# A deformable convolution stack on one core: window and offset loads re-laid, sums and residual once per band

## Chip, cores and metric

The kernel runs on 1 core of one Trainium2 chip. The metric is the device time of one launch in microseconds, lower is better; a time is the median of several runs.

## The reference

Eight images of 32 channels and 64 x 64 pixels are normalised, and pass through four blocks (a 3 x 3 convolution h = relu(conv(x)), a 3 x 3 convolution of h that gives 18 offsets per pixel, and a deformable convolution of h at these offsets), with residuals between the blocks. A final deformable convolution takes the result and the normalised input together (64 channels). All is float32.

```python
off = offset.reshape(Bn, K * K, 2, Hh, Ww)
py = base_y + off[:, :, 0]
px = base_x + off[:, :, 1]
sampled = jax.vmap(_bilinear_sample)(x, py, px)      # weights max(0, 1-|d|) of the four neighbours
return jnp.einsum('bckhw,ock->bohw', sampled, wk) + b
...
x = _block(x, deconv_w[0], ...)
in_prev = jnp.zeros_like(x)
for i in range(1, 4):
    in_cur = x + in_prev
    x = _block(in_cur, deconv_w[i], ...)
    in_prev = in_cur
x_cat = jnp.concatenate((x, in_module), axis=1)
offset = _conv2d(x_cat, fin_off_w, fin_off_b, PAD)
return _deform_conv2d(x_cat, offset, fin_dcn_w, fin_dcn_b)
```

## The kernel before

**Partition of the work.** The images are two groups of four; the 128 partitions are 4 images x 32 channels. Each of the four layers, and the final step, is done for one group after the other: ten steps in all. In a step the convolutions run first (`conv_tiles`, L467), the map h is transposed and stored to DRAM as `ht_store` (row, column, channels of four images; L330), and the scaled positions (offset plus tap) go through `FOFF` to DRAM as `off_store` (L339). VectorE reduces the positions to their range, and flags choose the kind of sampling: kind 0 (windows of 11 x 11 positions) ran in the eight steps of the layers, kind 1 (16 x 16 positions in two tiles of 128) in the two final ones. Then comes the call of sampling (`sampling`, L241), between barriers of all five engines.

**A call of sampling.** An image is 16 bands of 4 rows, a band two chunks of 32 columns (`half` 0 and 1), so 32 chunks; a chunk is 8 blocks of 4 x 4 pixels. `chunk_loop` (L254) writes the first and the last chunk out and loops over pairs of chunks between them. The bilinear weights are made as hats of a distance, and sampling becomes a matrix product of a window (positions on the partitions) with the weights of all its positions. Per chunk:

- SP loads the positions: `load_offsets` (L348), eight transfers per band for both halves, each to 16 partitions (`HB`), the source repeated 16 times. `load_windows` (L357) loads 11 transfers per chunk (16 in the final steps), one per window row, from `ht_store` to `VT`, in runs of 128 numbers (256 in the final steps).
- ScalarE: the distance |HB - position| of the next chunk (L693), VectorE clamps it (L844), GpSimd splits it into two fp16 hats (L998, L1000) that TensorE will read as `HL`.
- For each of 12 groups (three taps of one image), TensorE spreads the x hats and the y hats over the window positions (`spread`, L492, two matmuls each, times two tiles for y in kind 1) into the PSUM banks `P[2*slot]` and `P[2*slot+1]` of three slots; ScalarE copies x to `XC` (L707), VectorE multiplies y by it into `A` (L828).
- In between, TensorE samples the chunk before (`sample`, L505, matmuls of `A` and `VT` into one of the two banks of `PS`, two blocks per part); ScalarE reads each part into `SMP` (L676). After the last part the sums over the nine taps (`deform`, L523) run in two pieces, 128 columns wide; ScalarE applies bias and activation into `TMP` (L665), VectorE adds the residual into `X` (L822).

**What sets the order.** Each engine's program is written out by hand with semaphores. PE runs in order: `self.after` says after which group the parts of the chunk before are sampled, `self.sum_spots` where the pieces of the sums stand. PE may be at most three groups ahead of VectorE (`product_done`, credit of `SLOTS`). SP's queue is in order as well: in the loop over bands it waits until the second half of `HB` has been read, issues the eight offset loads of the next band, then waits for `ps_full` and issues the windows of the two chunks.

```python
src = bass.AP(off_store.ap().tensor, at, [[0, ROWS], [CH * CPX, 2], [1, TAPS * CPX]])
q = CH * i + ROWS * axis
sp.dma_start(HB[q:q + ROWS, :, :], src).then_inc(hb_full, 16)
```

"Units" are the two halves of the rows in the convolutions; "a part" is one sampling product group; "spread" means the matmul of the selection table `SEL` with the hats.

Of the kernel before, what the change touches and what calls it, by code (L numbers as in the profile page):

```python
# [14 lines left out]
IMG = 4  # L15
# [14 lines left out]

MARGIN = 6
HP = SIDE + 2 * MARGIN

XSIZE = (SIDE + 2) * HP
ROWS = 16
# [8 lines left out]

SHEETS = UNIT_ROWS * HP // 128
BANKFULS = (SHEETS + 3) // 4
# [7 lines left out]

class Shape:

    def __init__(self, kind, sources):
# [4 lines left out]

        self.batches = 2 if kind == 1 else 1
# [5 lines left out]
        self.parts = [(w, s) for w in range(0, self.blocks, 2) for s in range(sources)]  # L71

        runs = [2, 5] if len(self.parts) < 8 else [1, 3, 5, 7]
        count = len(self.parts) // len(runs)
        self.after = {g: list(range(count * n, count * (n + 1))) for n, g in enumerate(runs)}
        self.sum_spots = [8, 10] if len(self.parts) < 8 else [9, 10]

        self.read_after = {g + 1 + k: n for g in runs for k, n in enumerate(self.after[g])}
        self.out_after = 11
        self.ps_uses = self.batches * len(self.parts) + 1  # L80
        assert self.ps_uses % 2 == 1 and len(self.read_after) == len(self.parts)

def build(nc, t):

    ctx = ExitStack()
    with ctx:
# [3 lines left out]
        def sem(name):  # L91
# [5 lines left out]
        ht_store = [nc.dram_tensor(f"ht_store{n}", (HP, HP, n, 128), F32) for n in (1, 2)]  # L97

        SLOTS = 3  # L100
# [4 lines left out]
        XC = sb("XC", [128, SLOTS, 3 * CPX])  # L105
        SMP = sb("SMP", [128, 2, 2, TAPS * CPX])
        TMP = sb("TMP", [128, 2, CPX])
# [17 lines left out]
        P = ctx.enter_context(nc.psum_tensor("P", [128, 6, 512], F32))  # L125
        PS = ctx.enter_context(nc.psum_tensor("PS", [128, 2, 512], F32))
# [32 lines left out]
        hb_full = sem("hb_full")  # L159
# [3 lines left out]
        hats_full = sem("hats_full")  # L163
        x_full = sem("x_full")
        x_ready = sem("x_ready")
        y_full = sem("y_full")
# [7 lines left out]
                    flag_step, hb_full, abs_done, clamp_done, hat_step, hats_full, x_full, x_ready, y_full, product_done,  # L174
                    *vt_full, ps_full, ps_free, res_done, turn]

        credit = [(x_ready, SLOTS), (product_done, SLOTS), (y_full, 1), (ps_full, 2), (ps_free, 2), (res_done, 2), (turn, 1)]
# [13 lines left out]
        def bankful(unit, n):  # L191

            return SHEETS * unit + 4 * n, min(4, SHEETS - 4 * n)

# [4 lines left out]
        def bank(n):  # L199
            return P[:, n, :] if n < 6 else PS[:, n - 6, :]  # L200
# [8 lines left out]
        def smp_px(buf, source, w, blocks):  # L209
            return SMP[:, buf, source, 144 * w:144 * (w + blocks)]  # L210

# [17 lines left out]
        BARS = 4  # L229
# [11 lines left out]
        def sampling(eng, bar_count, final, body, fallback, clears=False):  # L241
# [5 lines left out]
            with eng.If(kind == 1):  # L247
                body(Shape(1, sources))
            with eng.If(kind > 1):
                fallback(Shape(2, sources))  # L250
            barrier(eng, bar_count + 1)
            clear_step(eng, bar_count + 2, clears)
# [36 lines left out]
        def _(sp):  # L289
# [40 lines left out]
            def store_ht(sources, s, unit, n):  # L330
                sp.wait_ge(ht_copied, (UNITS * s + unit) * BANKFULS + n + 1)
                first, count = bankful(unit, n)
                at = (MARGIN * HP + 128 * first) * sources * 128 + 128 * s
                dst = bass.AP(ht_store[sources - 1].ap().tensor, at,
                              [[sources * 128, 128], [128 * sources * 128, count], [1, 128]])
                sp.dma_start(dst, staged(s)[:, 128 * first:128 * (first + count)].rearrange(
                    "p (t c) -> p t c", c=128)).then_inc(ht_stored, 16)
# [761 lines left out]
```

## Time and profile before

| | us |
|---|---|
| median of 3 runs | 6885.23 |
| lowest, highest | 6860.79, 6908.06 |
| the profiled execution | 6814.77 |
| its span | 6813.0 |

| engine | busy us (share) |
|---|---|
| PE matmuls | 5270.7 (77%) |
| PE weight loads | 3746.3 (55%) |
| DVE (VectorE) | 2989.2 (44%) |
| ACT (ScalarE) | 2803.4 (41%) |
| POOL (GpSimd) | 1134.7 (17%) |

The granted clock of TensorE is 0.796 of the full one over the span. The span is the time from the first to the last instruction; the profiled execution's own time is a little longer. "Busy" is the time in which an engine executed; a line as "L693" is a line of the kernel; "<-" names what an engine's idle time ended with. "issue" is idle time that ends with no releaser in the profile. SPq is the queue in which SP issues transfers. In a window, PEclk is the granted clock as a share of the full one and "DMA share" the mean busy share of the 16 DMA engines (it can pass 1 where packets overlap).

### The profile page before, as it was taken

To read this page: it belongs to the slowest core of one execution; us is meant where nothing else is said; L and a number is where in the kernel's file an instruction comes from. 1 tells how busy PE (TensorE), PEld (TensorE's weight loads), DVE (VectorE), ACT (ScalarE), POOL (GpSimd) and SP (SyncE) were. 2 spreads that over 40 slices of the span, in tenths; PEclk is the share of its full clock that TensorE was granted. 3 is DMA by queue.
4 is the path that set the end of the run, shared out by engine and by line. 5 is a ranking of instruction groups with operands and counts; after the bars stand their busy time and mean duration, and the time that the engine had idled before them with its cause. 6 is when DMAs were issued, how large, how long until landed. Compare 5 with 4: busy or idle time off the path is not lost.

```text
span 6813.0 us, 210332 instructions
## 1 busy us (share of the span) xinstructions
PE 5270.7 (77%) x73160; PEld 3746.3 (55%) x73160; DVE 2989.2 (44%) x5831; ACT 2803.4 (41%) x7035; POOL 1134.7 (17%) x655
## 2 busy tenths in 40 slices
PE   3888688688688768868858868876777777678887
PEld 2555455355455545545535545554656566566776
DVE  3444454355355345445535534533334342344444
ACT  1554354255355345435525525542323232233333
POOL 0221222122022122112202202211101010111110
PEclk8778787688788878878868877887788788788888
DMA  5553553355255255345435525547666665778875
GB/s 152 75 75 56 79 80 60 70 80 81 56 77 79 57 79 78 55 81 81 71 65 78 78 56 77 77 91 106 78 77 84 79 80 83 116 91 96 96 90 77
DMA packets 615113, 544.03 MB, mean 80 GB/s; under 512 B 90160, under 2 KB 570160, under 8 KB 613040
## 3 DMA queue, kind: packets, MB, share of 16 engines
q1 hardware_dynamic: 614576, 536.57, 53.3%
q8 instruction: 374, 6.13, 0.5%
q14 instruction: 163, 1.34, 0.1%
HBM read 468.16 MB, written 68.12 MB: 79 GB/s over the span
## 4 chain that ended last, share of the span: by engine, by line
PE 51%; issue 21%; DMA 12%; ACT 6%; SPq 4%; DVE 3%; ACTq 1%; POOL 1%; POOLq 0%; PEldq 0%; PEld 0%; DVEq 0%
PE P L502 20%; PE PS L516 17%; PE PS L528 13%; DMA HB<-off_store 11%; SPq L355 4%; ACT SMP L676 2%; DVE A L828 2%; ACT XC L707 2%; ACT DIST L693 2%; PE P L474 1%; ACTq L704 0%; DMA H<-gn_store 0%; DMA gn_store<-X 0%; POOL HL L1000 0%; DMA X<-x_dram 0%
## 5 line engine op out<-in xcount | busy, mean ns | idle before, releaser
L828 DVE TENSOR_TENSOR A<-P,XC 121x384 f32<-121x384 f32 (+1 forms) x4608 | 2412.5, 555 | 3006.6 <-ACT XC L707 1595.6
L707 ACT ACTIVATE XC<-P 121x384 f32<-121x384 f32 (+1 forms) x4608 | 1961.1, 443 | 2903.3 <-PE P L502 2876.1
L502 PE MATMUL P<-HL,SEL 32*121 32x384 f16 (+1 forms) x21504 | 2355.4, 345 | 835.7 <-POOL HL L1000 393.6
L502 PEld LDWEIGHTS P<-HL,SEL 32*121 32x121 f16 (+1 forms) x21504 | 1341.2, 132 | 1632.7 <-issue 879.8
L516 PE MATMUL PS<-A,VT 121*32 121x144 f32 (+1 forms) x32768 | 1467.0, 335 | 124.1 <-issue 95.1
L516 PEld LDWEIGHTS PS<-A,VT 121*32 121x32 f32 (+1 forms) x32768 | 1098.5, 127 | 468.4 <-issue 238.0
L528 PE MATMUL PS<-SMP,CW 128*128 128x128 f32 x6912 | 1100.3, 316 | 301.7 <-ACT SMP L676 300.9
L528 PEld LDWEIGHTS PS<-SMP,CW 128*128 128x128 f32 x6912 | 963.6, 219 | 529.5 <-ACT SMP L676 428.2
L998 POOL CAST HL<-DIST 128x1152 f16<-128x1152 f32 x320 | 366.2, 1144 | 4394.1 <-DVE DIST L844 4110.0
L1000 POOL TENSOR_TENSOR HL<-DIST,HL 128x1152 f16<-128x1152 f32 x320 | 760.0, 2375 | 129.7 <-issue 73.9
L676 ACT ACTIVATE SMP<-PS 128x288 f32<-128x288 f32 x1536 | 639.2, 416 | 24.0 <-PE PS L516 22.7
L693 ACT ACTIVATE DIST<-HB,CONST 128x1152 f32<-128x1152 f32 x320 | 402.8, 1259 | 593.8 <-DMA HB<-off_store 593.7
L844 DVE TENSOR_SCALAR DIST<-DIST 128x1152 f32<-128x1152 f32 x320 | 240.2, 751 | 161.7 <-ACT DIST L693 161.7
L474 PE MATMUL P<-X,DW 32*32 32x512 f32 x3456 | 165.5, 682 | 158.6 <-DMA CW<-dcn_w_dram 120.3
L474 PE MATMUL P<-H,OW 32*32 32x512 f32 x3456 | 227.8, 684 | 35.1 <-DVE FOFF L927 35.1
L769 ACT ACTIVATE H<-P,BIAS 32x512 f32<-32x512 f32 x128 | 87.9, 686 | 258.5 <-PE P L474 225.6
L474 PEld LDWEIGHTS P<-H,OW 32*32 32x32 f32 x3456 | 131.3, 110 | 110.9 <-issue 80.1
L474 PE MATMUL PS<-H,OW 32*32 32x512 f32 x2304 | 189.0, 719 | 0.0
L474 PEld LDWEIGHTS P<-X,DW 32*32 32x32 f32 x3456 | 80.6, 109 | 193.8 <-issue 179.7
L1006 POOL PARTITION_ALL_REDUCE ST<-ST x10 | 3.9, 391 | 1088.3 <-DVE ST L950 1088.3
L927 DVE SCALAR_TENSOR_TENSOR FOFF<-P,PXB 128x512 f32<-128x512 f32 x48 | 32.9, 685 | 299.6 <-PE PS L474 188.6
L822 DVE SCALAR_TENSOR_TENSOR X<-X,CONST,TMP 128x128 f32 (+1 forms) x320 | 110.6, 346 | 65.5 <-ACT TMP L665 65.5
(55 smaller groups left out, 826.4 us busy)
## 6 DMA issues: line engine op xcount, KB each, us to landing
HB<-off_store SPq DMA_DIRECT2D x1280, 144.0 KB, 5.7
VT<-ht_store SPq DMA_DIRECT2D x1024, 128.0 KB
VT<-ht_store SPq DMA_DIRECT2D x2816, 44.0 KB
ht_store<-A SPq DMA_DIRECT2D x80, 256.0 KB, 3.6
off_store<-FOFF SPq DMA_DIRECT2D x160, 128.0 KB, 2.5
ht_store<-H SPq DMA_DIRECT2D x6, 1444.0 KB, 19.4
A<-x_dram SPq DMA_DIRECT2D x2, 2048.0 KB, 10.9
gn_store<-X SPq DMA_DIRECT2D x2, 2048.0 KB, 26.3
```

Source lines behind the costliest of these rows:

```text
L355: sp.dma_start(HB[q:q + ROWS, :, :], src).then_inc(hb_full, 16)
L474: mm = nc.tensor.matmul(bank(bank0 + i)[CH * j:CH * (j + 1), :], weights[q, CH * k:CH * (k + 1)], view(row + k // 3 - 1, col + k % 3 - 1)[ ...
L502: mm = nc.tensor.matmul(dst, SEL[q, table, 0:sh.npos], hats, start=part == 0, stop=part == 1)
L516: mm = nc.tensor.matmul(out[q, 144 * v:144 * v + 144].rearrange("p (k y x) -> p k y x", k=TAPS, y=BLK), vt_tile(sh, vt_buf, n, 0 if same_w ...
L528: mm = nc.tensor.matmul(out[:, 0:CPX], CW[:, s, 128 * k:128 * (k + 1)], rhs, start=n == 0, stop=n == len(products) - 1)
L676: nc.scalar.activation(smp_px(0, s, b * sh.blocks + w, 2), PS[:, (half + use) % 2, 0:288], ACT.Copy).then_inc(ps_free, 1)
L693: nc.scalar.activation(DIST[:, :], HB[:, half, :], ACT.Abs, bias=HAT_BIAS).then_inc(abs_done, 1)
L707: nc.scalar.activation(XC[0:sh.npos, slot, 0:sh.size], P[0:sh.npos, 2 * slot, 0:sh.size], ACT.Copy).then_inc(x_ready, 1)
L828: return nc.vector.tensor_tensor(dst, y, x, ALU.mult)
L844: nc.vector.tensor_scalar(DIST[:, :], DIST[:, :], SCALE, SCALE, ALU.min, ALU.subtract).then_inc(clamp_done, 1)
L998: nc.gpsimd.tensor_copy(HL[:, 0, half, :], DIST[:, :]).then_inc(hat_step, 1)
L1000: nc.gpsimd.tensor_tensor(HL[:, 1, half, :], DIST[:, :], HL[:, 0, half, :], ALU.subtract).then_inc(hats_full, 1)
```

## The change

- **Windows.** `ht_store` is laid out in four lanes: columns 0, 4, 8, ... of the padded map in the first, 1, 5, 9, ... in the second, and so on. The eight blocks of a chunk are four columns apart, so a window position's eight values are now one contiguous run (1024 numbers, 2048 in the final steps). A chunk's windows are four transfers, one per lane. The positions stand on the partitions in the order of lanes, and the tables `REL` and `SEL` follow. The transposes of h write lanes (20 instead of 19 per unit).
- **Offsets.** The y axis has 16 rows of the store and the x axis the next 16, so that one transfer per image and half fills 32 partitions of `HB`; its source is 2 axes x 16 repeats x 1152 numbers. Each half has its own semaphore, and the load of a chunk is issued when the distance two chunks earlier has run. The first band's loads, its first distance, clamp and hats stand ahead of the barrier of the step; they are issued after the first unit's offsets are stored, ahead of the stores of the second unit.
- **PSUM.** Three banks for the operand that ScalarE copies (now y) and four for the one that VectorE reads (now x), one bank for samples and sums instead of two.
- **Parts and sums.** Three parts per chunk of 3, 3 and 2 blocks (kind 0) instead of four of 2; six parts instead of eight in the final steps. Sums, activation and residual run once per band, over both chunks: 9 products of 256 columns (18 in the final steps), after group 10 of the first chunk of the next band.
- One barrier less per step, and nested branches instead of three in a row.

```diff
-            def load_offsets(band):
+            def load_offsets(band, half):
                 for i in range(IMG):
-                    for axis in range(2):
-                        at = band * BAND_SIZE + (i * 2 * CH + axis * TAPS) * CPX
-                        src = bass.AP(off_store.ap().tensor, at, [[0, ROWS], [CH * CPX, 2], [1, TAPS * CPX]])
-                        q = CH * i + ROWS * axis
-                        sp.dma_start(HB[q:q + ROWS, :, :], src).then_inc(hb_full, 16)
+                    at = band * BAND_SIZE + (2 * i + half) * CH * CPX
+                    src = bass.AP(off_store.ap().tensor, at, [[AXIS * CPX, 2], [0, AXIS], [1, TAPS * CPX]])
+                    sp.dma_start(HB[CH * i:CH * (i + 1), half, :], src).then_inc(hb_full[half], 16)
-            def load_windows(sh, buf, corner):
-                for r in range(sh.win):
-                    tile, first = divmod(r, sh.win // sh.tiles)
-                    src = bass.AP(ht_store[sh.sources - 1].ap().tensor, corner + r * (HP * sh.sources * 128),
-                                  [[sh.sources * 128, sh.win], [BLK * sh.sources * 128, BLOCKS], [1, sh.sources * 128]])
...
+            def load_windows(sh, buf, corners):
+                width = sh.sources * 128
+                size = BLOCKS * width
+                for corner, (tile, first, columns) in zip(corners, sh.lanes):
+                    src = bass.AP(ht_store[sh.sources - 1].ap().tensor, corner, [[LANE_COLS * width, sh.win], [width, columns], [1, size]])
+                    sp.dma_start(VT[first:first + sh.win * columns, buf, tile * size:(tile + 1) * size], src).then_inc(vt_full[buf], 16)
...
-                load_offsets(0)
-                load_windows(sh, 0, corner(0, 0))
-                with sp.Fori(0, BANDS - 1) as band:
-                    sp.wait_ge(abs_done, 2 * band + 2)
-                    load_offsets(band + 1)
-                    free_windows(2 * band + 1)
-                    load_windows(sh, 1, corner(band, 1))
-                    free_windows(2 * band + 2)
-                    load_windows(sh, 0, corner(band + 1, 0))
+                load_windows(sh, 0, corners(0, 0))
+                load_windows(sh, 1, corners(0, 1))
+                next_offsets(2, 1, 0)
+                next_offsets(3, 1, 1)
+                with sp.Fori(0, BANDS - 2) as pair:
+                    next_offsets(2 * pair + 4, pair + 2, 0)
+                    next_windows(pair + 1, 0)
+                    next_offsets(2 * pair + 5, pair + 2, 1)
+                    next_windows(pair + 1, 1)
...
+                    if unit == 0:
+                        for slot in range(OFF_SLOTS):
+                            sp.wait_ge(off_stored[slot], 32)
+                        load_offsets(0, 0)
+                        load_offsets(0, 1)
...
-        P = ctx.enter_context(nc.psum_tensor("P", [128, 6, 512], F32))
-        PS = ctx.enter_context(nc.psum_tensor("PS", [128, 2, 512], F32))
+        P = ctx.enter_context(nc.psum_tensor("P", [128, Y_SLOTS + X_SLOTS, 512], F32))
+        PS = ctx.enter_context(nc.psum_tensor("PS", [128, 512], F32))
...
+                    rhs = SMP[:, first:first + chunks, 0:sh.smp_size].rearrange(
+                        "p h (w s k a) -> p h w s k a", s=sh.sources, k=TAPS, a=BPX)[:, :, :, s, k, :]
+                    mm = nc.tensor.matmul(PS[:, 0:chunks * CPX], CW[:, s, 128 * k:128 * (k + 1)], rhs,
...
+                distance(0, 0)
                 sampling(act, bar_count, final, lambda sh: body_of(sh, final), lambda sh: fallback_of(sh, final))
...
                 for n in range(ITEMS):
                     unit, image = divmod(n, IMG)
+                    if n == IMG:
+                        clamp(0)
```

SP, in the loop over bands of a layer's sampling, before; a row is one instruction with the shape of its destination, `ISA` a register or wait instruction:

```order
L355 ISA [waits abs_done]
L355 DMA HB<-off_store 16x2x1152
...
L380 ISA
L364 ISA [waits ps_full]
L364 DMA VT<-ht_store 11x8x128
```

The same place now:

```order
L372 ISA [waits abs_done]
L372 DMA HB<-off_store 32x1x1152
...
L402 ISA
L380 ISA [waits ps_full]
L380 DMA VT<-ht_store 33x1x1024
```

The eight offset loads of a band, in one piece, became four for each half, each four with a wait of its own and the windows of one chunk behind them; the eleven windows became four (three of 33 partitions and one of 22).

PE, in the first chunk of the loop, one part of samples between two groups of spreads, and a piece of the sums, before:

```order
L516 MATMUL PS<-A,VT 32x144 [waits ps_free]
L516 MATMUL PS<-A,VT 32x144 x7
L564 REGISTER_ALU
...
L528 MATMUL PS<-SMP,CW 128x128 [waits ps_free]
L528 MATMUL PS<-SMP,CW 128x128 x3
L564 REGISTER_ALU
```

Now, in the second chunk of the loop:

```order
L549 MATMUL PS<-A,VT 32x144 [waits ps_free]
L549 MATMUL PS<-A,VT 32x144 x11
...
L583 REGISTER_ALU
L562 MATMUL PS<-SMP,CW 128x256 [waits ps_free]
L562 MATMUL PS<-SMP,CW 128x256 x8
L590 REGISTER_ALU
```

A part is now three blocks in 12 matmuls, and the sums of both chunks stand in one piece of nine, where each chunk had a piece of four and one of five.

## Rows read from the trace of the kernel before

**Rows 1.** Distances (L693) of three sampling calls: count, ns min/median/max, first to last start.

```profile
L693 ACT ACTIVATE DIST<-HB,CONST x32: 1246/1255/1282, 2958.6 to 3388.7; 128x1152 f32<-128x1152 f32 x32
...
L693 ACT ACTIVATE DIST<-HB,CONST x32: 1245/1251/1256, 4644.3 to 5688.7; 128x1152 f32<-128x1152 f32 x32
...
L693 ACT ACTIVATE DIST<-HB,CONST x32: 1246/1251/1256, 5850.6 to 6740.1; 128x1152 f32<-128x1152 f32 x32
```

**Rows 2.** Windows, one period of four chunks in a layer.

```profile
core 0: us, PE busy (x) PEld busy (x) DVE busy (x) ACT busy (x) POOL busy (x), PEclk, DMA share, GB/s
3093.90:3128.10 34.20, 28.89 (x360) 19.40 (x356) 19.42 (x39) 21.93 (x52) 7.68 (x5) 1.00 0.67 92
3128.10:3148.50 20.40, 19.29 (x168) 12.19 (x165) 9.39 (x19) 8.79 (x21) 6.56 (x4) 0.50 0.32 59
```

**Rows 3.** Timeline of the same chunks, ACT and SP: start, us, what [idle before].

```profile
3100.94 1.27 ACT L693 ACTIVATE DIST<-HB,CONST 128x1152 f32<-128x1152 f32 x1
...
3112.24 1.27 ACT L693 ACTIVATE DIST<-HB,CONST 128x1152 f32<-128x1152 f32 x1
...
3113.70 3.83 SPq L355 DMA_DIRECT2D HB<-off_store  x8
...
3125.35 1.25 ACT L693 ACTIVATE DIST<-HB,CONST 128x1152 f32<-128x1152 f32 x1 [1.66 <-DMA HB<-off_store]
...
3141.49 1.25 ACT L693 ACTIVATE DIST<-HB,CONST 128x1152 f32<-128x1152 f32 x1
```

**Rows 4.** Timeline of one chunk at the full clock, PE.

```profile
3104.24 1.19 PE L516 MATMUL PS<-A,VT 121*32 121x144 f32 x32
...
3107.46 1.16 PE L528 MATMUL PS<-SMP,CW 128*128 128x128 f32 x8 [1.09 <-ACT SMP L676]
...
3109.35 1.38 PE L528 MATMUL PS<-SMP,CW 128*128 128x128 f32 x10
3110.66 0.89 PE L502 MATMUL P<-HL,SEL 32*121 32x384 f16 x12
```

**Rows 5.** Timeline in the first final call, SP and PE.

```profile
5142.88 9.28 SPq L364 DMA_DIRECT2D VT<-ht_store  x16
...
5164.22 4.05 PE L516 MATMUL PS<-A,VT 128*32 128x144 f32 x59 [9.15 <-issue]
```

**Rows 6.** Waits of PE in the two final calls: us, times, longest.

```profile
PE P L502 <- issue: 148.6, 29, 9.0
PE PS L516 <- issue: 89.4, 12, 9.4
...
PE P L502 <- issue: 107.5, 15, 11.3
```

**Rows 7.** Windows with offset loads, loads of x, and window loads (final).

```profile
3114.50:3125.00 10.50, 9.12 (x122) 6.26 (x124) 6.68 (x14) 5.73 (x15) 3.52 (x2) 1.00 0.99 128
13.00:24.00 11.00, 0.00 (x0) 0.00 (x0) 10.63 (x18) 0.20 (x1) 0.00 (x0) 1.00 1.02 398
5143.00:5161.00 18.00, 11.07 (x175) 9.24 (x170) 6.45 (x13) 4.76 (x17) 0.00 (x0) 0.94 1.12 122
```

**Rows 8.** The page, DMA packets and the issues of the loads.

```profile
DMA packets 615113, 544.03 MB, mean 80 GB/s; under 512 B 90160, under 2 KB 570160, under 8 KB 613040
...
HB<-off_store SPq DMA_DIRECT2D x1280, 144.0 KB, 5.7
VT<-ht_store SPq DMA_DIRECT2D x1024, 128.0 KB
VT<-ht_store SPq DMA_DIRECT2D x2816, 44.0 KB
```

**Rows 9.** Timeline between two calls of sampling, before the first chunk.

```profile
3496.39 0.69 DVE L927 SCALAR_TENSOR_TENSOR FOFF<-P,PXB 128x512 f32<-128x512 f32 x1 [11.57 <-PE PS L474]
...
3510.10 3.63 SPq L355 DMA_DIRECT2D HB<-off_store  x8
...
3521.18 1.25 ACT L693 ACTIVATE DIST<-HB,CONST 128x1152 f32<-128x1152 f32 x1 [41.06 <-DMA HB<-off_store]
```

More of the change, by code:

```diff
@@ L53 @@
 BAND_SIZE = IMG * 2 * CH * CPX
+AXIS = 16
 class Shape:
@@ L63, in __init__ @@
         self.npos = self.win * self.win // self.tiles
+        if kind == 0:
+            self.lanes = [(0, 33 * j, 3 if j < 3 else 2) for j in range(LANES)]
+        else:
+            self.lanes = [(j // 2, 64 * (j % 2), 4) for j in range(LANES)]
         self.batches = 2 if kind == 1 else 1
@@ L70, in __init__, with use @@
         self.size = 3 * self.px
[L71 to L81, printed above, removed]
+        units = [(w, s) for w in range(self.blocks) for s in range(sources)]
+        count = {4: 2, 8: 3, 16: 6}[len(units)]
+        edges = [(len(units) * n + count - 1) // count for n in range(count + 1)]
+        self.parts = [units[a:b] for a, b in zip(edges, edges[1:])]
+        self.after = {2: [3, 7], 3: [2, 5, 8], 6: [0, 2, 4, 5, 7, 8]}[count]
+        self.sum_after = 10
+        self.chunk_uses = self.batches * count
+        self.band_uses = 2 * self.chunk_uses + 1
+        self.smp_size = BLOCKS * sources * TAPS * BPX
+    def use(self, band, half, n=0):
+        return band * self.band_uses + half * self.chunk_uses + n
 def build(nc, t):
@@ L158, in build @@
         flag_step = sem("flag_step")
-        hb_full = sem("hb_full")
+        hb_full = [sem(f"hb_full{i}") for i in range(2)]
         abs_done = sem("abs_done")
@@ L246, in sampling @@
                 body(Shape(0, sources))
[L247 to L252, printed above, removed]
+            with eng.Else():
+                with eng.If(kind == 1):
+                    body(Shape(1, sources))
+                with eng.Else():
+                    fallback(Shape(2, sources))
+            clear_step(eng, bar_count + 1, clears)
         def chunk_loop(eng, body, tail):
@@ L503, in spread, with sample @@
                 return mm
-            def sample(sh, a_buf, vt_buf, first, w, source, out, same_window=False):
-                for v in range(2):
+            def sample(sh, a_buf, vt_buf, first, units, same_window=False):
+                for v, (w, source) in enumerate(units):
                     for n in range(sh.tiles):
@@ L695, in body, with read_sum, next_distance @@
+                def read_sum(band):
+                    act.wait_ge(ps_full, sh.use(band, 2) + 1 + PS_CREDIT)
+                    act.wait_ge(res_done, band + 2)
+                    out_act(final, 2 * BLOCKS).then_inc(ps_free, 1)
+                def next_distance(c, band, half):
+                    wait_alone(act, hats_full, c)
+                    distance(band, half)
                 def body(c, band, half, first, last):
-                    if first:
-                        distance(0, 0, 0, True)
@@ L867, in body @@
                                 clamp(c + 1)
-                            if not first and b == sh.batches - 1 and g == (11 if sh.kind == 0 else 1):
-                                add_residual(c - 1, band + half - 1, 1 - half)
+                            if half == 0 and not first and b == sh.batches - 1 and g == (11 if sh.batches == 1 else 1):
+                                add_residual(band - 1)
                 def tail():
-                    add_residual(CHUNKS - 1, BANDS - 1, 1)
+                    add_residual(BANDS - 1)
                 chunk_loop(dve, body, tail)
```

334 lines of the change are left out of this document (164 added, 170 removed).

## The prediction

> **What bounds the kernel now.** I read the start times of the distance step first, because there is one per chunk and so they are a clock of the work; then the windows of one period, the waits, and the DMA views. A layer's call of sampling takes 430.1 us from its first distance to its last, 31 chunks of 13.9 us. The two final calls take 1044.4 and 889.5 us, 33.7 and 28.7 us a chunk [rows 1]. Eight calls of the first kind are 3,440 us, the two final ones 1,934: sampling is four fifths of the 6813 us.
>
 At the full clock a chunk takes 11.3 us, in which PE has four groups of spreads of 0.89, two of samples of 1.19 and two of sums of 1.16 and 1.38, together 8.5 us [rows 4]; the rest is PE waiting for ScalarE and VectorE, for instance 1.09 us ahead of the sums.
>
> In the final calls PE stops for 5 to 11 us at a time with nothing named as releaser, 238.0 us in the first call and 107.5 in the second [rows 6]. The stop that ends at 5164.22 after 9.15 us lies at the end of window loads that were issued from 5142.88 on [rows 5]; they carry 16 times 128 KB, and at the 122 GB/s of that window this is 17 us [rows 7, 8]. I read these stops as PE's own instructions arriving late behind the window data.
>
> **The offset loads.** This is the largest term, and it speaks against the change. Before, a band takes eight loads of 16 by 2 by 1152, now each chunk takes four of 32 by 1152, with a source whose outer count is 2 (the two axes), then 16 repeats. The bytes are the same, 590 KB a chunk. How many of the 16 DMA engines share a transfer can be counted. Each transfer ends with one 4-byte write per engine. There are 5443 transfers: 1280 of offsets, 1024 and 2816 of windows [rows 8], 323 others. If each ended on 16 engines, there would be 87,088 such writes; if the 2816 whose rows are 11 on both sides end on 11, there are 73,008. Add the other short packets (16,384 of 256 B from the two stores of x, 768 of constants) and it is 90,160, exactly the count under 512 B [rows 8]. So a transfer is dealt out by its outer count. No transfer of before has a 2 there. Dealt by the source's count of 2, the new loads run on two engines; dealt by the destination's 32, on sixteen. I take two, since an engine can't be given part of an outer step in any transfer that I can count. The Trainium skill, in DMA: Bandwidth & Descriptors, section Why a DMA increments its semaphore by 16 and not by 1, says that the number is the largest up to 16 that divides the outer sizes of both sides, and that it is the lowest-numbered engines; by that it is two, always the same ones. The count above agrees for 11 and 16 and shows nothing of 2 against 32.
>
> What two engines give: while x is loaded, 16 engines move 398 GB/s, 24.9 each; in an offset load of before all 16 move 128 GB/s, 8.0 each, all of them on one source row at a time [rows 7]. Two engines alone ask for 50 GB/s, far under the 128, so I take 24.9 and keep 8.0 as the far end. Each of the two carries 64 runs of 4608 B per chunk, and of the windows 11 runs of 4096 B (three columns in three loads, two in the last), 340 KB. That is **13.7 us a chunk** at 24.9 GB/s, 42 us at 8.0. It is double-buffered by halves: the load of a chunk is issued when the distance two chunks earlier has run, so the two engines are never without work. SP is not in the way: it issues 8 transfers a chunk instead of 15, and its wait for a distance holds back only windows that are needed a chunk later. The distances then follow each other at 13.7 us, whatever PE could do.
>
> **What else the layers gain, and what hides it.** The sums run once per band with 256 columns instead of twice with 128: between no gain (columns decide) and 2.5 us per band (weight loads decide); three reads of PSUM instead of four, one activation and one residual per band instead of two; four product slots instead of three, so that PE's samples no longer stop VectorE. Without transfers I would put a chunk at 10.3 us at the full clock, between PE's 8.5 and the 11.3 of now. All of it lies under the 13.7 us of the two engines and is worth nothing there. At half the clock PE needs up to 17 us for a chunk and could be last again for a chunk, but it catches up afterwards, so the mean stays near 13.7; I allow 0.8 us for it in the range. Waits of 3 us per chunk will keep the clock falling.
>
> Per layer call: the chunk-0 distance and hats are now ahead of the barrier. Before, loads were issued at 3510.10 and that distance ran at 3521.18 [rows 9], PE some 5 us later. But the two halves of band 0 take 2 x 11.8 us on two engines, VectorE's clamp of chunk 0 now stands ahead of the second unit's offsets (3496.39 now [rows 9]), and the second unit's stores queue behind them. I put the start of PE at about 3522 instead of 3526, a gain of 4 of a possible 13. The load for chunk 2 lands some 18 us later (3.6 of windows, 11.8 of offsets, 2 of start), at 3540; 29 more at 13.7 bring the last distance to 3937, 416 us after where the first one was, against 430. With 4 us for the last chunks and one barrier less, a call saves 18 us: **8 x 18 = 144 us**.
>
> **The final calls.** Chunks are 24 us and more, so 11.8 us of offsets don't bind. The windows of a chunk come in four transfers with runs of 8 KB instead of 16 with 1 KB. On all 16 engines the 2 MB take 17 us now [rows 7]; at between 398 and half of that they take 5 to 11. If fetched instructions wait behind them, stops of 9 us shrink to the 3 to 4 us of the shortest. The first call has 41 stops for 238 us, the second 15 for 107.5 [rows 6]. Saved per call, at 3.5 us each that stay: 94 and 55 us, and a third as much again in less time at the low clock; sums, reads and the wider ring give 1 to 1.5 us of a 24 us chunk, some 40 us per call. **280 us** for both, between 80 (stops stay) and 450 (they vanish).
>
> **Sum.** The profiled execution took 6814.8 us (span 6813.0). Less 144, 280 and 10 for the two final starts, it gives 6381. The median of the runs is 6885.2, 70 above the profiled one: **6450 us**.
>
> **Rivals.** (1) The loads are spread over 16 engines after all. Then a chunk's 725 KB take 5.7 us at 128 GB/s, hidden; no distance waits, the clock stays up, and a layer chunk takes 10.6 us: 3.3 us less for 248 chunks is 820, the starts give 100 more, the final calls 350: 6885 - 1270 = 5615. For it: the destination has 32 rows; against it: the count of 11. (2) Slower: the two engines are slower than 24.9 GB/s on these runs, with the same DRAM rows read 16 times, as the 8.0 in a crowd shows. It decides from 15.5 us a chunk (21.9 GB/s), where 1.8 us more for 248 chunks has eaten the 434. At 18 us a chunk it costs 4.3 x 248 = 1070: 7520. (3) The stops in the final calls are not from the window data and stay: 200 us of the gain are gone, 6650. (4) The stop at the low clock feeds itself, and a layer chunk takes 14.8: 6450 + 270 = 6720.
>
> **Chances.** Forecast 0.50, (1) 0.14, (2) 0.13, (3) 0.12, (4) 0.11. The likeliest case has 6250 to 6650 for itself. To leave out at most 2 in 10 the range reaches to 5750 and to 6950. About 1% can be told from no change here. Faster by more than 1%: 0.80, within 1%: 0.06, slower: 0.14.
>
> **What would show it.** Right: 4-byte writes for the offset loads that count 2 each, distances 13.5 to 14 us apart in the layers with waits for HB of 2 to 4 us ahead of nearly every one, a DMA share of all 16 engines under 0.3 there, and PE and VectorE idle behind ScalarE; in the final calls, stops under 5 us. The forecast is wrong if the distances of a layer come under 12 us or over 15, or if the waits for HB are gone.

## The result, and the profile after

| | before | after |
|---|---|---|
| median, us (4 runs each) | 6873.01 | 6303.22 |
| lowest to highest | 6830.16 to 6908.06 | 6294.74 to 6315.18 |
| profiled execution, us | 6814.77 | 6309.22 |
| mean granted clock | 0.796 | 0.798 |

The ratio is 0.9175, with a 95% interval of 0.9118 to 0.9232: the kernel became 8% faster. Some executions of a kernel fall into a slower state with a lower granted clock; ratios here and below are of the other executions alone, so they are not always the quotient of two medians. The two profiled executions differ by 505.5 us; the prediction had 434.

The distances of the same three calls as in [rows 1], now L698:

```profile
L698 ACT ACTIVATE DIST<-HB,CONST x32: 1247/1258/1284, 2854.6 to 3285.2; 128x1152 f32<-128x1152 f32 x32
...
L698 ACT ACTIVATE DIST<-HB,CONST x32: 1245/1255/1288, 4488.9 to 5383.9; 128x1152 f32<-128x1152 f32 x32
...
L698 ACT ACTIVATE DIST<-HB,CONST x32: 1245/1262/1292, 5512.5 to 6236.0; 128x1152 f32<-128x1152 f32 x32
```

The layer's call shown still takes 430.6 us for 31 chunks, where it took 430.1; over the eight calls the mean chunk went from 14.0 to 13.9 us. The final calls fell from 1044.4 and 889.5 us to 895.0 and 723.5.

The page, DMA packets and the issues of the loads, against [rows 8]:

```profile
DMA packets 233565, 542.39 MB, mean 86 GB/s; under 512 B 40240, under 2 KB 141360, under 8 KB 215216
...
HB<-off_store SPq DMA_DIRECT2D x1280, 144.0 KB
VT<-ht_store SPq DMA_DIRECT2D x256, 512.0 KB
VT<-ht_store SPq DMA_DIRECT2D x768, 132.0 KB
VT<-ht_store SPq DMA_DIRECT2D x256, 88.0 KB
```

The count of short packets settles how the offset loads are dealt out. With two closing writes for each of the 1280 loads, 11 for the 1024 window loads of the layers (768 and 256), 16 for the 256 of the final calls and for the 323 others, there are 23,088; with the 17,152 short packets of x and the constants this is 40,240, the number of the page. So each offset load runs on two engines. The rule of the Trainium skill that the prediction named (DMA: Bandwidth & Descriptors, section Why a DMA increments its semaphore by 16 and not by 1) is borne out for 2 against 32, which no transfer of before could show. Which two engines they are, no view shows.

The DMA view of 50 us in a layer call. Each digit is the busy share of the 16 engines in tenths, under it what they moved:

```profile
DMA  4211111114452111111124441111111544111111
GB/s 149 98 52 52 52 52 52 52 49 143 141 153 91 52 52 52 52 52 51 52 78 152 132 157 52 52 52 52 52 50 52 154 141 157 68 52 52 52 55 52
```

No slice is empty. Between the window loads the strip stands at 1 tenth, two engines of 16, at 52 GB/s: 26 each. In the trace's records of packets some load is in flight at every moment of this call after its first 32 us. This queue doesn't run dry.

One would now expect ScalarE to wait ahead of each distance. It doesn't. The timeline of ScalarE, SP and PE in some chunks of the same call (start, us, what, idle before):

```profile
3018.29 1.26 ACT L698 ACTIVATE DIST<-HB,CONST 128x1152 f32<-128x1152 f32 x1
...
3031.38 1.27 ACT L698 ACTIVATE DIST<-HB,CONST 128x1152 f32<-128x1152 f32 x1
...
3043.15 1.25 ACT L698 ACTIVATE DIST<-HB,CONST 128x1152 f32<-128x1152 f32 x1 [3.10 <-DMA HB<-off_store]
...
3045.09 1.67 PE L549 MATMUL PS<-A,VT 121*32 121x144 f32 x24 [4.74 <-DMA VT<-ht_store]
...
3054.97 5.60 PE L562 MATMUL PS<-SMP,CW 128*128 128x256 f32 x18 [0.23 <-ACT SMP L707]
...
3062.18 1.28 ACT L698 ACTIVATE DIST<-HB,CONST 128x1152 f32<-128x1152 f32 x1
...
3070.75 1.25 ACT L698 ACTIVATE DIST<-HB,CONST 128x1152 f32<-128x1152 f32 x1
```

The distances follow at 13.1, 11.8, 19.0 and 8.6 us. A wait for offsets comes once in several chunks:

```profile
ACT DIST L698 <- DMA HB<-off_store: 355.6, 62, 21.1
```

In the call shown it is 37.8 us in seven waits, 21.1 of them ahead of the first distance. There is a new wait: PE waits 4.74 us for windows (105.2 us in 68 waits in the whole run). I read these as windows that queue behind the offsets on the two engines; with the offsets over 16 engines, below, no such wait is left. The windows of three whole chunks:

```profile
3062.20:3070.80 8.60, 7.53 (x113) 5.09 (x112) 7.17 (x14) 7.25 (x18) 3.53 (x2) 1.00 0.17 64
3070.80:3089.10 18.30, 16.72 (x133) 10.60 (x130) 7.12 (x15) 7.63 (x19) 3.52 (x2) 0.63 0.26 88
2963.80:2976.90 13.10, 11.95 (x133) 8.22 (x131) 7.04 (x15) 7.57 (x19) 3.53 (x2) 1.00 0.25 82
```

A chunk without sums takes 8.6 us at the full clock, one with sums 13.1 at the full clock or 18.3 when the clock is granted at 0.63. Two answers therefore fit a mean of 13.9: the two engines' queue, or the clock. The experiments are for that.

### The profile page after: what moved, and what is told of

The parts are those of the page before. It is cut to its first block, busy times and chain, and to the rows that moved or that the text cites. A ratio compares the mean times of both kernels' runs of the same rounds, so it can differ in the third digit from the quotient of the medians.

```text
span 6307.3 us, 193915 instructions
## 1 busy us (share of the span) xinstructions
PE 5045.6 (80%) x69728; PEld 3538.5 (56%) x69728; DVE 2954.9 (47%) x5671; ACT 2709.2 (43%) x6491; POOL 1135.4 (18%) x655
## 2 busy tenths in 40 slices
DMA packets 233565, 542.39 MB, mean 86 GB/s; under 512 B 40240, under 2 KB 141360, under 8 KB 215216
## 4 chain that ended last, share of the span: by engine, by line
PE 53%; DMA 14%; SPq 12%; issue 9%; ACT 7%; DVE 2%; POOL 2%; ACTq 1%; POOLq 0%; DVEq 0%
PE PS L549 20%; PE P L535 16%; PE PS L562 13%; DMA VT<-ht_store 9%; ACT SMP L707 5%; SPq L380 5%; PE P L506 4%; SPq L372 3%; SPq L355 3%; DMA HB<-off_store 2%; ACT YC L730 1%; POOL HL L1018 1%; SPq L364 1%; DMA off_store<-FOFF 1%; ACT H L791 1%
## 5 line engine op out<-in xcount | busy, mean ns | idle before, releaser
L851 DVE TENSOR_TENSOR A<-P,YC 121x384 f32<-121x384 f32 (+1 forms) x4608 | 2386.0, 553 | 2560.4 <-ACT YC L730 1738.1
L730 ACT ACTIVATE YC<-P 121x384 f32<-121x384 f32 (+1 forms) x4608 | 1858.2, 447 | 2678.9 <-PE P L535 2661.7
L535 PE MATMUL P<-HL,SEL 32*121 32x384 f16 (+1 forms) x21504 | 2138.7, 341 | 551.3 <-issue 338.8
L549 PE MATMUL PS<-A,VT 121*32 121x144 f32 (+1 forms) x32768 | 1499.2, 329 | 409.4 <-ACT SMP L707 137.3
L549 PEld LDWEIGHTS PS<-A,VT 121*32 121x32 f32 (+1 forms) x32768 | 1027.8, 123 | 883.3 <-issue 411.7
L562 PE MATMUL PS<-SMP,CW 128*128 128x256 f32 x3456 | 995.9, 456 | 50.1 <-ACT SMP L707 50.1
L562 PEld LDWEIGHTS PS<-SMP,CW 128*128 128x128 f32 x3456 | 791.9, 234 | 265.9 <-ACT SMP L707 126.1
L707 ACT ACTIVATE SMP<-PS 128x432 f32<-128x432 f32 (+1 forms) x1152 | 563.2, 489 | 53.1 <-PE PS L549 53.1
L698 ACT ACTIVATE DIST<-HB,CONST 128x1152 f32<-128x1152 f32 x320 | 404.4, 1264 | 355.8 <-DMA HB<-off_store 355.6
L845 DVE SCALAR_TENSOR_TENSOR X<-X,CONST,TMP 128x256 f32 (+1 forms) x160 | 77.4, 483 | 142.4 <-ACT TMP L691 136.3
L936 DVE TENSOR_SCALAR H<-P,BIAS 32x512 f32<-32x512 f32 x96 | 72.0, 750 | 144.9 <-PE P L506 116.4
## 6 DMA issues: line engine op xcount, KB each, us to landing
A<-x_dram SPq DMA_DIRECT2D x2, 2048.0 KB, 10.3
```

What stands on the lines that cost most here:

```text
L535: mm = nc.tensor.matmul(dst, SEL[q, table, 0:sh.npos], hats, start=part == 0, stop=part == 1)
L549: mm = nc.tensor.matmul(PS[q, 144 * v:144 * v + 144].rearrange("p (k y x) -> p k y x", k=TAPS, y=BLK), vt_tile(sh, vt_buf, n, 0 if same_wi ...
L562: mm = nc.tensor.matmul(PS[:, 0:chunks * CPX], CW[:, s, 128 * k:128 * (k + 1)], rhs, start=n == 0, stop=n == len(products) - 1)
L698: nc.scalar.activation(DIST[:, :], HB[:, half, :], ACT.Abs, bias=HAT_BIAS).then_inc(abs_done, 1)
L707: nc.scalar.activation(smp_px(half, sh, b * sh.blocks + w, s, count), PS[:, 0:TAPS * BPX * count], ACT.Copy).then_inc(ps_free, 1)
L730: nc.scalar.activation(YC[0:sh.npos, g % X_SLOTS, 0:sh.size], P[0:sh.npos, g % Y_SLOTS, 0:sh.size], ACT.Copy).then_inc(y_ready, 1)
```

## Experiments

The ratio of each is to the kernel before, run beside it on the same chip. The medians of that kernel beside them lay between 6796 and 6870 us, so a difference of about 1% between runs of different sets can't be told.

### Offset loads over 16 engines

```diff
-                    src = bass.AP(off_store.ap().tensor, at, [[AXIS * CPX, 2], [0, AXIS], [1, TAPS * CPX]])
-                    sp.dma_start(HB[CH * i:CH * (i + 1), half, :], src).then_inc(hb_full[half], 16)
+                    for axis in range(2):
+                        src = bass.AP(off_store.ap().tensor, at + axis * AXIS * CPX, [[0, AXIS], [1, TAPS * CPX]])
+                        q = CH * i + AXIS * axis
+                        sp.dma_start(HB[q:q + AXIS, half, :], src).then_inc(hb_full[half], 16)
```

> The changed kernel with each offset load split by axis: eight transfers per half whose source and destination both have 16 rows. Against the changed kernel (6303). Theory Q (the two engines' queue sets the mean of the layers' chunks near 13.9 us): the queue is gone, waits for HB fall below 50 us in all, a layer chunk comes to 10.8 us (the 8.57 and 13.08 of the pairs that run at the full clock) and a call's 31 distances to some 335 us instead of 431; 8 calls save 770, so about 5530 us. Theory C (the low clock after the stretch of sums sets it, and the loads are a side matter): HB waits vanish too, but a band keeps alternating between about 21.7 and 27 us, the mean is 12.2 or more, a call about 378, and the total 5850 or more. The short packets in the page: 40240 + 2560 x 0 - 2560 + 2560 x 16 = 78640 if the new loads end on 16 engines each.

Measured: 5841.46 us, ratio 0.8621 (0.8545 to 0.8697). Of this kernel the page, the distances of the same call, ScalarE's wait for offsets, and windows of three chunks:

```profile
DMA packets 271974, 542.62 MB, mean 93 GB/s; under 512 B 78640, under 2 KB 179760, under 8 KB 253616
```

```profile
L700 ACT ACTIVATE DIST<-HB,CONST x32: 1247/1264/1286, 2528.8 to 2922.4; 128x1152 f32<-128x1152 f32 x32
```

```profile
ACT DIST L700 <- DMA HB<-off_store: 131.8, 11, 14.1
```

```profile
2626.00:2639.00 13.00, 11.84 (x132) 8.20 (x130) 6.98 (x14) 7.47 (x18) 3.53 (x2) 1.00 0.37 112
2639.00:2647.60 8.60, 7.54 (x114) 5.06 (x112) 7.12 (x15) 7.27 (x17) 3.52 (x2) 1.00 0.30 83
2718.80:2736.70 17.90, 17.03 (x133) 10.88 (x131) 7.06 (x14) 7.60 (x18) 3.52 (x2) 0.62 0.27 82
```

The short packets are 78,640, as worked out. Inside the layer calls the waits for offsets are gone (ten of the 11 left are those of the starts), no wait of PE for windows is left, and the mean over the eight calls falls from 13.9 to 12.4 us a chunk. So the queue was the bound, and it cost 6 to 7% of the run. But theory Q's 10.8 us doesn't come: nine of the call's 15 chunks with sums still take about 18 us at a clock of 0.62. Under the queue lay a second bound only 1.5 us lower, the clock.

### Sums once per chunk, with the loads as changed and over 16 engines

```diff
-                            if phalf == 1 and pb == sh.batches - 1 and g == sh.sum_after:
-                                sums(pband)
+                            if pb == sh.batches - 1 and g == sh.sum_after:
+                                sums(pband, phalf)
```

Sums and activation are 128 columns wide and run once per chunk; the residual stays once per band. First with the loads on two engines:

> The changed kernel with the sums once per chunk (128 columns) after group 10 of the next chunk, each with its own activation; the residual stays once per band. Theory Q: the queue's 13.9 us a chunk stays, calls of 430 us, total within 1% of 6303. Theory C: a stretch of sums is half as long, VectorE and ScalarE idle less in one piece, the clock falls less often; the granted clock rises above 0.80, a call comes to 400 us or less, total about 6060.

Then with both edits:

> Offset loads over 16 engines and sums once per chunk. Theory Q: as with the loads alone, 10.8 us a chunk plus what the doubled sums cost (nine matmuls more and one read more per band, 1 to 2 us a band), so slower than the loads alone by 100 to 200 us, some 5650. Theory C: faster than the loads alone, since the clock no longer falls, about 5550 against 5850.

Measured: 6251.20 us, ratio 0.9233 (0.9159 to 0.9306), and 5736.26 us, ratio 0.8469 (0.8383 to 0.8555). The distances of a call in the one and in the other:

```profile
L704 ACT ACTIVATE DIST<-HB,CONST x32: 1246/1257/1280, 2816.4 to 3247.4; 128x1152 f32<-128x1152 f32 x32
```

```profile
L706 ACT ACTIVATE DIST<-HB,CONST x32: 1247/1266/1286, 2529.4 to 2905.8; 128x1152 f32<-128x1152 f32 x32
```

```profile
core 0: 6258.6 us, clock 0.839
```

```profile
core 0: 5759.4 us, clock 0.887
```

On two engines the clock rose from 0.798 to 0.839, and the call took 431.0 us all the same, where theory C had 400 or less. That agrees with the queue as the bound, but this pair of runs doesn't separate the two theories. On 16 engines the clock rose as well, from 0.850 to 0.887, and the call shown takes 376.4 us instead of 393.6, yet over the eight calls the mean chunk only went from 12.36 to 12.27 us, as it went from 13.94 to 13.86 on two engines; both profiled executions became 49 us shorter. The reason is in the band, here with both edits:

```profile
2684.70:2695.80 11.10, 9.96 (x132) 6.93 (x131) 7.29 (x15) 7.44 (x18) 3.53 (x2) 1.00 0.33 97
2695.80:2707.00 11.20, 10.12 (x132) 7.12 (x131) 6.96 (x15) 7.55 (x19) 3.53 (x2) 1.00 0.36 99
```

Where no low clock falls into it, it takes 22.25 us instead of 21.65, since the nine products of 256 columns take 4.15 us and two times nine of 128 take 2 x 2.27, and there is one read more. The better clock pays for that and little more.

By the medians the edit is worth 1.8% on 16 engines (5699 to 5761 us against 5810 to 5851, on one chip). On two engines its sign can't be told: the median is 0.8% lower, the ratio to the kernel before 0.6% higher. Theory C had the order right on 16 engines and hoped for too much: 5550 us. The sums once per band, part of the change, are thus no gain here. With both edits the first final call fell to 794.6 us and the second rose to 802.7; the loads alone had 884.2 and 707.6.

### The band's products in two stretches

```diff
+                for n in range(count * piece[0] // piece[1], count * (piece[0] + 1) // piece[1]):
...
+                            if phalf == 1 and pb == sh.batches - 1 and g in (sh.sum_after - 1, sh.sum_after):
+                                sums(pband, g - sh.sum_after + 1, 2)
```

> The offset loads over 16 engines as in the run before (5841, layers 12.4 us a chunk, a sums chunk of 13.1 us or 17.9 to 18.3 us), and the band's nine products in two stretches, four after group 9 and five after group 10, with a group of spreads between. If it is the 4.2 us stretch of sums, in which ScalarE and VectorE run dry and PE then waits for them, that brings the clock down, the chunks of 18 us become rare, a layer call comes to 31 x 10.9 = 338 us instead of 390, the granted clock rises from 0.85 to 0.9 or more, total about 5450. If the amount of sums work decides and not its place, the alternation of 21.7 and 26.7 us a band stays and the total is within 1% of 5841.

Measured: 6175.86 us, ratio 0.8974 (0.8946 to 0.9001), clock 0.808: a miss in the other direction. The two windows of a band at the full clock:

```profile
2978.50:2992.60 14.10, 12.93 (x134) 8.56 (x131) 7.05 (x14) 7.70 (x19) 3.53 (x2) 1.00 0.36 103
2992.60:3001.20 8.60, 7.53 (x113) 5.09 (x112) 7.18 (x14) 7.26 (x18) 3.53 (x2) 1.00 0.30 84
```

The band grew by 1.0 us at the full clock, which explains some 125 us of the 335 (240 by the ratios); the rest is a clock that was low in more places and for longer (12 stretches and 215 us of one call, against 9 and 164), with chunks of 19 and 22 us. My reason for the falls, the length of one stretch of sums, is refuted: two stretches of half the length with one group between them are worse, although they are better when they are a chunk apart.

### Three slots for x instead of four, loads over 16 engines

```diff
-        Y_SLOTS, X_SLOTS = 3, 4
+        Y_SLOTS, X_SLOTS = 3, 3
```

> The run with loads over 16 engines (5841), with the x product slots at three banks instead of four as in the kernel before (one bank stays unused). If the fourth slot is what brought a chunk without sums to 8.57 us, that chunk takes 9 us or more and the total rises by 120 us or more; if PE, ScalarE and VectorE are each at their own rate there, less than 1% changes.

Measured: 6182.53 us, ratio 0.9134 (0.9064 to 0.9204), clock 0.812. A band at the full clock:

```profile
2882.20:2895.80 13.60, 12.45 (x134) 8.29 (x134) 7.25 (x14) 7.73 (x19) 3.53 (x2) 1.00 0.38 112
2895.80:2904.50 8.70, 8.23 (x108) 4.75 (x108) 6.84 (x14) 7.07 (x17) 3.53 (x2) 1.00 0.25 78
```

Neither theory had it: the chunk without sums moves by 0.1 us, so the slot is hardly seen there, yet the run is 341 us longer. The two chunks of a band are 0.6 us longer at the full clock, some 80 us over the eight calls. In the profiled executions these calls lose 234 us and the two final ones 73, so the larger part again came with the lower clock (0.850 to 0.812).

### The kernel before, with its loads on two engines

```diff
-                    for axis in range(2):
-                        at = band * BAND_SIZE + (i * 2 * CH + axis * TAPS) * CPX
-                        src = bass.AP(off_store.ap().tensor, at, [[0, ROWS], [CH * CPX, 2], [1, TAPS * CPX]])
-                        q = CH * i + ROWS * axis
-                        sp.dma_start(HB[q:q + ROWS, :, :], src).then_inc(hb_full, 16)
+                    for half in range(2):
+                        at = band * BAND_SIZE + (i * 2 + half) * CH * CPX
+                        src = bass.AP(off_store.ap().tensor, at, [[TAPS * CPX, 2], [0, ROWS], [1, TAPS * CPX]])
+                        sp.dma_start(HB[CH * i:CH * (i + 1), half, :], src).then_inc(hb_full, 16)
```

> The kernel before with one change: a band's eight offset loads are issued as 32 by 1152 per image and half (source: 2 axes, 16 repeats), same bytes, same issue point. If a transfer with the outer counts 2 and 32 runs on two engines, a band's loads take 128 x 0.18 = 23 us on them instead of 8 to 10 us on 16, all at the band's end and in no overlap with the band before: the third distance of each four waits 13 us or more, a layer call goes from 430 to at least 500 us, and the total to 7400 or more. If the kernel before stays within 2% of itself, the two engines cost nothing by themselves.

Measured: 9042.64 us, ratio 1.3378 (1.3257 to 1.3498). ScalarE's wait, and two distances of one band:

```profile
ACT DIST L692 <- DMA HB<-off_store: 2946.1, 160, 78.7
```

```profile
4368.74 1.27 ACT L692 ACTIVATE DIST<-HB,CONST 128x1152 f32<-128x1152 f32 x1
4370.20 6.51 SPq L354 DMA_DIRECT2D HB<-off_store  x8
...
4398.63 1.25 ACT L692 ACTIVATE DIST<-HB,CONST 128x1152 f32<-128x1152 f32 x1 [18.42 <-DMA HB<-off_store]
```

The direction was right, and the size was far above my bound. From the issue to the distance are 28.4 us for a band's offsets, each band, because before nothing is loaded ahead of the last distance of a band. So the changed kernel's double buffer by halves, loaded two chunks ahead, is what makes the two engines bearable: the same loads cost 34% in the old order and 6 to 7% in the new one.

### The kernel before, with a quarter of the window rows in the final calls

```diff
-                for r in range(sh.win):
+                for r in range(sh.win) if sh.kind == 0 else (0, 1, 8, 9):
```

A clearing of the window buffer at the start goes with it. The kernel leaves out three quarters of the window data there, so the values that it samples are wrong; it is for the time alone. In the text below L501 and L515 stand for L502 and L516 of this kernel.

> The kernel before, with only 4 of the 16 window rows loaded in the two final calls (the sampled values there come from what lies in the buffer, so this leaves out three quarters of the window data; layers unchanged). If PE's stops of 5 to 11 us in the final calls last as long as the window loads fill the engines, the windows now fill them for 4 to 5 us instead of 17, the stops fall to 3 us (the length they have in the changed kernel), the issue waits of L501 and L515 in the two calls from 345 to about 150 us, and the calls from 1044 and 890 us to about 900 and 800; total about 6640. If the stops have another reason they stay at 5 to 11 us and the total within 1% of before.

Measured: 6454.31 us, ratio 0.9544 (0.9491 to 0.9597). The distances of the two final calls, and the longest kind of stop that is left:

```profile
L693 ACT ACTIVATE DIST<-HB,CONST x32: 1245/1251/1257, 4597.8 to 5418.2; 128x1152 f32<-128x1152 f32 x32
...
L693 ACT ACTIVATE DIST<-HB,CONST x32: 1245/1250/1259, 5580.8 to 6374.2; 128x1152 f32<-128x1152 f32 x32
```

```profile
4736.85 1.73 PE L502 MATMUL P<-HL,SEL 32*128 32x192 f16 x18 [3.62 <-issue]
```

```profile
PE P L502 <- issue: 50.4, 14, 3.9
...
PE P L502 <- issue: 30.8, 15, 5.0
```

The waits of the two calls were 148.6 and 107.5 us at the spreads and 89.4 us at the samples of the first [rows 6]; 81 us are left, none longer than 5.0. The waits fell by 264 us, and the calls by 224.0 and 96.1; the clock was also up more of the time (0.90 and 0.89 in the two calls, against 0.79 and 0.85). The window data did hold PE up.

|---|---|---|---|
| before | 53 | -0.7 to 6.1 | 1.2 to 2.6 |
| before, a quarter of the rows | 21 | 0.2 to 0.7 | 1.4 to 2.4 |
| after, first call | 11 | 0.1 to 0.7 | 1.4 to 1.9 |

Every stop ends shortly after a fetch ended. In the kernel before, the 36 stops of over 5 us have window loads in flight, and the fetch begins 2.1 to 6.1 us into them; nine stops with no load in flight have it after 0.2 to 1.2 us and last 3.1 to 3.9. So a short stop is a fetch by itself, and a long one is a fetch that comes late while window data is moving.

### Windows of the final calls in runs of 1 KB

```diff
+                        for b in range(BLOCKS):
+                            src = bass.AP(ht_store[sh.sources - 1].ap().tensor, corner + b * width, [[LANE_COLS * width, sh.win], [width, columns], [1, width]])
```

> The changed kernel with the windows of the two final calls loaded block by block: 32 transfers of runs of 1 KB for each chunk instead of 4 of runs of 8 KB, same bytes and places; the layers are untouched. If short runs in the window loads are what holds up PE in the final calls of the kernel before, its stops of 5 to 11 us return: PE's issue waits at the spreads and samples, 338.8 and 93.0 us in the changed kernel, rise by 150 us or more, and the two final calls take 895 and 723 us plus 75 or more each; total about 6450 to 6600. If the stops went for another reason (the smaller number of instructions, the wider ring), the final calls stay within 20 us each and the total within 1% of 6303.

Measured: 6485.25 us, ratio 0.9434 (0.9414 to 0.9454). SP's queue in the second final call, and PE's waits in it:

```profile
5755.24 23.00 SPq L385 DMA_DIRECT2D VT<-ht_store  x32
```

```profile
PE PS L555 <- DMA VT<-ht_store: 103.5, 14, 8.6
```

The time is in the range that I gave for short runs, but not for that reason. Issuing 32 transfers takes SP 23.0 us a chunk, 0.72 each, the windows arrive late, and PE waits for them by name. The two calls take 29.6 and 149.4 us more than in the changed kernel, and the stops with nothing named as releaser didn't come back: 337.9 us at the spreads in all, against 338.8, and 61.2 at the samples, against 93.0, though with one of 12 us ahead of the first samples of each final call. The engines never fill as they did before (DMA share 0.37 in this call against 1.12 [rows 7]). So it isn't the number of transfers that makes the stops. This run prices many small transfers, some 180 us, and leaves open whether few transfers with runs of 1 KB would bring the stops back.

## Why the prediction was right, and where not

The forecast of 6450 us with a range of 5750 to 6950 held, and so did its sign. Of the 147 us between forecast and median, half is a gain that came out larger, below; the other half is the 70 us that I had added because the median lay above the profiled execution. After the change it lies 6 us below. The profiled difference of 505.5 us is made up as follows, from PE's first spread of a call to its last distance, and from there to the next first spread:

| | forecast | measured |
|---|---|---|
| eight layer calls with their starts | 144 (calls 80, starts 64) | 130 (calls 66, starts 64) |
| two final calls | 280 | 357 |
| two final starts | 10 | 17 |
| the end | 0 | 2 |

**Two engines.** Right, by the count of short packets, and shown by the run over 16 engines. The price was right too: 13.7 us forecast, 13.9 measured, a mean that the clock alone would have put at 12.4. The engines gave 26 GB/s each in the long stretches rather than 24.9; that the mean came out longer all the same I put down to the windows among them, which no run shows by itself.

**Waits ahead of nearly every distance.** Wrong. The step that failed is "the distances then follow each other at 13.7 us": that is the mean, not the spacing. The chunks take 8.6, 13.1 or 18.3 us on their own account, the double buffer evens these out, and only 355.6 us of waits in 62 places are left, fewer than before (593.7 in 92). More than half of either sum stands at the ten starts. Part of the bound shows elsewhere, as PE's waits for windows behind offsets (105.2 us). A reader of the list of waits alone would have called the offsets a side matter.

**10.3 us hidden under it.** The two chunks of a band take 21.65 us at the full clock, 10.8 each, near the forecast. PE's part in it was read too low: not 8.5 us a chunk but 9.7 (11.84 and 7.54 in the two windows on 16 engines). But rival (1) took that number for what would come out without the queue, with "the clock stays up". It did not: 12.4 us and 5841, where the rival had 10.6 and 5615. This was the rival's mis-sized term: the lower clock is granted with every wait for offsets gone.

**Rival (2)**, a slower queue from 15.5 us, is excluded by 26 GB/s. **Rival (4)**, a low clock that feeds itself, was right in that the clock stays low much of the time (ten stretches, 227 of the 431 us of the call shown) and wrong in the sum: 13.9 us a chunk, not 14.8. The short chunks catch up, as the forecast said.

**Starts.** From the last distance to the next first spread the forecast had 8 us per call, 4 for PE's earlier start and 4 for the last chunks and the barrier; 15 came in the first start and 7 on average in the others. On 16 engines it is 20 (from the last distance to PE's first spread 140.7 us before, 133.7 after, 120.7 on 16). ScalarE still waits 20 us for the first offsets, half of the 41.06 of [rows 9].

**Final calls.** The mechanism was right and rival (3) is refuted: with a quarter of the rows in the kernel before the stops shrink to 3 to 5 us and 320 us go. The size was off, and the mis-sized term is the stops: I gave them 149 us, and they fell by 215 (from 239 and 113 us to 120 and 17, starts left out). The rest, for which I had some 130 us (50 for the clock and 80 for sums, reads and the wider ring), measured 142. The two final calls as a whole, before and after:

```profile
4644.30:5688.70 1044.40, 760.40 (x12927) 628.53 (x12929) 398.73 (x780) 316.76 (x1018) 109.46 (x62) 0.79 0.68 81
5850.60:6740.10 889.50, 729.48 (x12924) 600.25 (x12924) 394.67 (x780) 314.28 (x1017) 109.27 (x62) 0.85 0.80 94
...
4488.90:5383.90 895.00, 717.44 (x12449) 572.51 (x12423) 403.67 (x794) 303.99 (x943) 109.59 (x63) 0.86 0.41 102
5512.50:6236.00 723.50, 647.00 (x12434) 530.84 (x12418) 401.96 (x794) 296.77 (x943) 109.54 (x63) 0.96 0.52 123
```

The clock rose from 0.79 and 0.85 to 0.86 and 0.96. How the 142 us divide between the clock and the other parts, no run separates. In the changed kernel the second call has no long stop left after its first chunks; the windows of two of them further on:

```profile
5695.50:5713.70 18.20, 17.51 (x248) 14.34 (x245) 7.82 (x16) 6.20 (x20) 3.52 (x2) 1.00 0.61 129
5713.70:5740.50 26.80, 25.42 (x591) 21.04 (x592) 18.36 (x37) 13.45 (x45) 3.53 (x2) 1.00 0.48 116
```

PE is busy for 42.9 of 45.0 us at the full clock: this stage is now at PE's own rate. The first call keeps stops of some 3 us:

```profile
4660.56 0.66 PE L535 MATMUL P<-HL,SEL 32*128 32x192 f16 x6 [3.13 <-issue]
```

**What stays open.** What decides whether the clock falls in a band. It is not the length of one stretch of sums, and it is not the waits for offsets. It isn't a band's time at the full clock either: bands of 21.65, 22.29 and 22.65 us came with clocks of 0.850, 0.812 and 0.808, but one of 22.25, with the sums a chunk apart, with 0.887. That the first final call keeps stops and the second doesn't goes with the number of fetches of 16 KB: 134 against 10, where before it was 131 against 62. Why the counts differ so, with the same instructions, is open. With the sums once per chunk and 16 engines they are 135 and 73, and there the first call is the faster one. Open is also the effect of 1 KB runs in few transfers.

The version with both edits, loads over 16 engines and sums once per chunk, takes 5736 us: a ratio to the kernel before of 0.847 where the change alone has 0.9175, so 8 to 9% below the changed kernel.

## What to carry to other kernels

Before a transfer is reshaped, count on how many engines it will run: loads of 16 rows became loads of 32 with an outer count of 2 in their source, and ran on an eighth of the engines. Where a bound is removed, look how far below it the next one lies: loads over 16 engines were to give 3 us a chunk and gave 1.5, because the clock came next. Compare all calls and not one: a call that was 17 us faster stood for eight whose mean gained 3. And a deep enough buffer hides a saturated queue from the list of waits; look for a DMA strip that never shows a zero.

## What I had not expected of the hardware

Small changes in a chunk's own time had large effects through TensorE's clock: one PSUM slot less moved a band by 0.6 us at the full clock and the run by 341, of which only some 80 are that time itself. The granted clock was 0.850 with it and 0.812 without. And the time that SP takes to issue a window load didn't follow its size: 0.72 us for 64 KB (32 in 23.0 us), 0.70 for 512 KB (4 in 2.80 us, the final calls of the changed kernel), 0.58 for 128 KB (16 in 9.28 us [rows 5]). So SP's queue itself can become the bound when transfers are many and small. And PE's own instructions are fetched by DMA too, 16 KB at a time: without window data in flight a fetch began 0.1 to 1.2 us into a stop and mostly took 0.9 to 1.4 us, with window data it began up to 6.1 us into it.
